# A graph attention layer on one core: the node table in two float32r parts instead of three bfloat16 parts, and one-hot rows made by VectorE

## The chip, the cores and the metric

The kernel runs on one core of a Trainium2 chip. The metric is the device time of one execution in microseconds (us), here the median of three runs. The core has TensorE (PE), VectorE (DVE), ScalarE (ACT), GpSimd (POOL) and SyncE (SP), each with a queue of its own that is worked off in order. SBUF is the working memory with 128 partitions, PSUM takes what TensorE computes. Indirect transfers (gathers and scatters by a list of row numbers) are issued by GpSimd, the others here by SyncE.

## What is computed

12500 nodes of 32 values, 400000 edges sorted by their destination. Two layers follow each other. Cut to what matters:

```python
# layer 0: messages from an edge network and the source's features, summed by destination
x = silu(silu(edge_radial @ W1 + b1) @ W2 + b2);  tpw = x @ W3 + b3
messages = concatenate([m0, m1])        # products of h[src], edge_sh and tpw
agg = segment_sum(messages, dst, num_segments=n_atoms) / sqrt(16)
x = layernorm(x + h_self + agg)
# layer 1: attention
s_src = h @ attn_w[:d];  s_dst = h @ attn_w[d:]
e = s_src[src] + s_dst[dst];  e = where(e >= 0, e, 0.01 * e)
ex = exp(e - segment_max(e, dst)[dst])
out = segment_sum(h[src] * (ex / denom[dst])[:, None], dst)
x = layernorm(x + out)
```

## The kernel before

The edges lie in 3125 tiles of 128, one edge of each tile per partition. Four stages follow each other.

1. The message stage, layer 0. 130 iterations of four groups of six tiles, and a rest. GpSimd gathers the source rows, one indirect transfer per tile (L402). TensorE runs the edge network in float32 (L490, L494, L501), ScalarE the activations, VectorE the products and sums (L808 to L882). In the first 101 iterations one more gather (`dst_row`) serves a search for the edges at which each node's run ends.
2. The node stage. GpSimd gathers 98 columns of sums (`agg0`), VectorE makes the layer norm in seven batches (L1037 to L1052), and after each batch GpSimd scatters 14 columns of attention terms (`starts`, L406), 98 in all. SyncE writes each batch of the new node rows (33 values: 32 features and `s_src`) to `table` in HBM. VectorE also splits each batch into three bfloat16 parts whose sum is the float32 value: high and middle in `xs`, low in `big`.
3. The attention stage, 125 blocks of 25 tiles. The rows of the sources of 20 tiles are gathered by GpSimd from `table`, one transfer of 128 rows each (`gather_block`). Those of the other five tiles are "found" by TensorE: the table lies in SBUF as 128 partitions by 98 nodes, in seven batches of 14 nodes. For each edge a one-hot column says in which partition its source node lies, for each of the seven batches. A matmul of the one-hot rows (128 x 128) with a batch's table part (128 x 462, that is 14 nodes of 33 values) puts the 14 candidates of each edge into PSUM, summed over 7 batches and 3 parts: 21 matmuls per tile, 105 per block (`find_rows`, L536 to L546). VectorE multiplies the 14 candidates by a mask that keeps one (L1079), and sums over them (L1087) into the ring where the gathered rows lie too.
   The one-hot rows are made by ScalarE (`one_hot`, L680 to L697): the square of the difference between the edge's slot number and the partition's (L688), then relu(1 - 2 x square) (L696), for 640 edges at a time and for each batch: 14 instructions per block. There are two copies of them (`hot[k]`), so block b+1's are made while TensorE reads block b's.
   VectorE then does the softmax part of the block (`softmax_block`, L1089 to L1133), with exponentials by ScalarE (L670 to L672), and running sums by scan instructions (L1131); ScalarE lays the result out (L677), SyncE stores it.
4. The last gathers of 98 columns (`agg1`) and the last layer norm.

What orders the attention stage are semaphores. `gather_block(b)` waits until the softmax of block b-2 has used its ring half (`ring_used`) and until the finds of block b-1 are complete (`found_ready`). `find_rows` of a tile waits for the one-hot rows (`hot_ready`) and for VectorE to have multiplied the same PSUM bank of the block before (`found_used`). VectorE's queue has `pick(b)`, then `softmax_block(b)`, which waits for the gathers of block b. Two transposes through TensorE (`turn`) stand ahead of the stage: VectorE needs their results for its last preparations (L1056 to L1065).

## Time and profile before

| | |
|---|---|
| median of three runs | 7700.68 us (7698.39 to 7708.93) |
| span of the profiled execution | 10226.3 us |
| the profiled execution's own time beside its span | the page gives none; the span stands for it |
| granted TensorE clock, mean | 0.737 |
| busy: PE, PE weight loads, DVE, ACT, POOL | 63%, 33%, 49%, 32%, 56% |
| DMA | 331.33 MB, 32 GB/s over the span |

The profiled execution is one run of the program with the hardware profiler on. Its busy shares are of 10226.3 us, not of 7700. "Idle before" in a row is the time for which the engine did nothing ahead of the instructions of that group, and the arrow names what ended it; "issue" means that the profile shows nothing that it waited for. The granted clock is given as a share of full speed: 0.50 is 1.2 GHz, 1.00 is 2.4 GHz. The message stage takes the first half of the span, the attention stage all from about 5370 to 10070 us.

### The profile page before, as it was taken

What the parts mean: (1) busy time and instruction counts of PE and PEld (TensorE: products, weight loads), DVE (VectorE), ACT (ScalarE), POOL (GpSimd) and SP (SyncE); (2) the same over time, 40 slices, a digit from 0 to 9 for tenths busy, and PEclk for the clock granted to TensorE, in tenths of its full rate; (3) what the DMA queues carried; (4) which work ended last, traced back from release to release, by engine and by line L of the source; (5) the groups of instructions that cost most, each with busy time, mean ns of one, the idle gap of its engine ahead of it and who ended that gap; (6) DMA issues with size and microseconds to landing.
All of it is one profiled execution on the core that took longest, in us unless ns stands there. A gap on an engine that the chain in (4) does not pass through costs nothing.

```text
span 10226.3 us, 80982 instructions
## 1 busy us (share of the span) xinstructions
PE 6469.2 (63%) x21671; PEld 3367.5 (33%) x21671; DVE 5013.5 (49%) x8628; ACT 3261.4 (32%) x4929; POOL 5757.4 (56%) x6031
## 2 busy tenths in 40 slices
PE   5666666666666666666516666666666666666662
PEld 3333333433333333434312222222222222222221
DVE  6676666667666666777633222222222222222222
ACT  2323232323323232222203333333333333333330
POOL 6666666666666666666565445555445554445555
PEclk7777777777777777777657777777777777777775
DMA  2111111111111111111101111111111111111111
GB/s 51 37 34 37 35 37 35 37 37 35 37 35 37 35 37 33 29 31 31 40 14 35 29 28 30 31 30 30 30 27 30 31 30 30 29 28 30 30 30 23
DMA packets 338423, 331.33 MB, mean 32 GB/s; under 512 B 184277, under 2 KB 279541, under 8 KB 337859
## 3 DMA queue, kind: packets, MB, share of 16 engines
q0 software_dynamic: 196032, 148.74, 11.5%
q1 hardware_dynamic: 142370, 182.39, 5.7%
q14 instruction: 16, 0.12, 0.0%
q8 instruction: 5, 0.08, 0.0%
HBM read 219.80 MB, written 110.86 MB: 32 GB/s over the span
## 4 chain that ended last, share of the span: by engine, by line
PE 37%; issue 29%; another core or an unknown queue 18%; ACT 7%; DVE 6%; DMA 1%; SPq 1%; ACTq 0%; POOL 0%; DVEq 0%; POOLq 0%
PE tpw L545 25%; PE hid L545 6%; ACT early L570 2%; PE hid L490 2%; ACT hid L564 2%; PE hid L494 2%; PE tpw L501 2%; DVE msgs L882 1%; DVE prod L817 1%; DVE red L829 1%; DVE early L829 1%; ACT hv L577 1%; ACT junk_row L593 1%; ACT early L581 1%
## 5 line engine op out<-in xcount | busy, mean ns | idle before, releaser
L402 POOL DMA_INDIRECT early<-in_x_wide,idx x3126 | 2991.1, 957 | 1919.2 <-DVE prod L817 988.5
L402 POOL DMA_INDIRECT prod<-table,idx x2500 | 2374.1, 950 | 2305.4 <-PE hid L545 1568.4
L545 PE MATMUL tpw<-xs,early 128*128 128x462 bf16 x7000 | 2221.3, 393 | 1048.5 <-issue 1038.5
L501 PE MATMUL tpw<-w3s,early 128*128 128x256 f32 x6252 | 2039.0, 492 | 54.5 <-DVE prod L817 53.8
L501 PEld LDWEIGHTS tpw<-w3s,early 128*128 128x128 f32 x6252 | 1521.3, 252 | 761.9 <-issue 353.9
L545 PE MATMUL tpw<-big,early 128*128 128x462 bf16 x3500 | 1383.6, 395 | 586.6 <-issue 585.9
L494 PE MATMUL hid<-hid,w2s 128*128 128x384 f32 x1044 | 633.2, 699 | 1742.4 <-ACT hid L564 1108.6
L1079 DVE TENSOR_TENSOR prod<-tpw,mask 128x462 f32<-128x462 f32 x500 | 319.8, 640 | 2729.9 <-remote 2185.4
L570 ACT ACTIVATE early<-hid,b2s 64x384 f32<-64x384 f32 x1044 | 602.3, 577 | 2905.0 <-remote 1857.9
L545 PEld LDWEIGHTS tpw<-xs,early 128*128 128x128 bf16 x7000 | 702.3, 101 | 2031.0 <-issue 1454.4
L808 DVE TENSOR_TENSOR prod<-tpw,early 128x1152 f32<-128x1152 f32 x521 | 704.7, 1353 | 886.0 <-remote 813.7
L670 ACT ACTIVATE tpw<-diff 128x25 f32<-128x25 f32 x125 | 24.4, 195 | 2623.5 <-DVE prod L1105 1268.0
L494 PEld LDWEIGHTS hid<-hid,w2s 128*128 128x128 f32 x1044 | 233.7, 253 | 1884.1 <-ACT hid L564 1198.1
L688 ACT ACTIVATE early<-early,bases 128x640 f32<-128x640 f32 x875 | 710.4, 827 | 21.4 <-issue 0.2
L545 PEld LDWEIGHTS tpw<-big,early 128*128 128x128 bf16 x3500 | 362.2, 103 | 1062.1 <-issue 787.1
L817 DVE TENSOR_TENSOR prod<-tpw,hv 128x1152 f32<-128x1152 f32 x521 | 701.3, 1346 | 0.0
L696 ACT ACTIVATE early<-early,bases 128x640 bf16<-128x640 f32 x875 | 700.0, 814 | 0.0
L490 PE MATMUL hid<-early,w1s 16*128 16x384 f32 x1046 | 666.0, 727 | 19.4 <-DMA early<-in_radial_t 10.5
L545 PE MATMUL hid<-xs,early 128*128 128x462 bf16 x1750 | 582.3, 420 | 0.2 <-issue 0.2
L617 ACT ACTIVATE sums<-msgs 128x768 f32<-128x768 f32 x131 | 274.5, 2095 | 652.2 <-DVE msgs L882 412.5
L790 DVE TENSOR_TENSOR bprod<-hv,big 128x288 f32<-128x288 f32 (+1 forms) x261 | 118.5, 454 | 648.8 <-ACT hv L577 407.4
L1087 DVE TENSOR_REDUCE prod<-prod 128x33 f32<-128x462 f32 x625 | 379.7, 624 | 0.0
(176 smaller groups left out, 5718.0 us busy)
## 6 DMA issues: line engine op xcount, KB each, us to landing
scan<-prod SPq DMA_DIRECT2D x125, 425.0 KB
early<-in_x_wide,idx POOLq DMA_INDIRECT x3126
scan<-sums SPq DMA_DIRECT2D x130, 384.0 KB
early<-qrows SPq DMA_DIRECT2D x126, 320.0 KB
prod<-table,idx POOLq DMA_INDIRECT x2500
early<-in_radial_t SPq DMA_DIRECT2D x262, 48.0 KB
big<-in_sh SPq DMA_DIRECT2D x131, 48.0 KB
idx<-in_src SPq DMA_DIRECT2D x262, 6.0 KB
```

The costliest lines, as they stand in the source:

```text
L402: return pool.indirect_dma_start(out=dest, out_offset=None, in_=source, in_offset=bass.IndirectOffsetOnAxis(ap=index, axis=0))
L490: pe.matmul(hid[:, 0, 0:HC], w1s[:, :], rad[:, k, :], start=True, stop=True).then_inc(layers_done, 1)
L494: pe.matmul(hid[:, 1, 0:HC], w2s[:, :], hid1[:, :], start=True, stop=True)
L501: mm = pe.matmul(tpw_v(b)[:, t, :], hid2[:, b, at:at + P], w3s[:, :], start=True, stop=True)
L545: mm = pe.matmul(found[i][:, 0:BC], hot[k][:, g, i * P:(i + 1) * P], split(s, g), start=g == 0 and s == 0, stop=g == NBATCH - 1 and s == S ...
L570: act.activation(hid2[0:HR, b, half * HC:(half + 1) * HC], hid[units, 1, 0:HC], ACT.Silu, bias=b2s[units, :])
L688: act.activation(near[g % 2], qb[k], ACT.Square, bias=near_bias[:, g:g + 1])\
L696: act.activation(hot[k][:, g, :], near[g % 2], ACT.Relu, scale=-2.0, bias=one)\
L808: dve.tensor_tensor(prod_a[b].rearrange("p (t w u) -> p t w u", t=GT, w=MUL), w[:, :, 0:3 * MUL * MUL].rearrange("p t (w u) -> p t w u", w ...
L817: dve.tensor_tensor(prod_b[b].rearrange("p (t i w u) -> p t i w u", t=GT, i=3, w=MUL), w[:, :, 3 * MUL * MUL:].rearrange("p t (w u) -> p t ...
L1079: dve.tensor_tensor(picked[i % 2], found[i][:, 0:BC].rearrange("p (w a) -> p w a", a=BJ), mask[:, k, i:i + 1, :].to_broadcast([P, TW, BJ]) ...
L1087: dve.tensor_reduce(ring[:, k, GT1 + i, :], picked[i % 2], AX, ALU.add).then_inc(picked_ready, 1)
```

## The change

- The table parts are two float32r tensors, `highs` and `lows`: the value rounded to float32r, and the rest. A tile needs 14 matmuls, a block 70.
- The one-hot rows are float32r too, made by VectorE: one comparison of the slot numbers with the partition's number (`is_equal`) per batch. There is one copy of them, in two pieces: tiles 0 to 2 (384 edges) and tiles 3 and 4 (256 edges). Each piece has a semaphore of its own. VectorE makes the first piece for block b+1 in `pick(b)` after the third tile's reduction, the second at the end of `pick(b)`; each waits until TensorE has finished with the piece (`found_ready`).
- ScalarE's one-hot instructions are gone.
- The first block's one-hot rows are made by VectorE right ahead of the loop; TensorE does its two transposes first and has one block per turn of its loop instead of two.
- Buffers of the first half (`xs`, `early`, `hid1` and others) share their places with those of the second (`lows`, `highs`, `hot`, `qb`). The slot numbers are computed in a late part of `big`, and SyncE waits for their store before it goes on.

```diff
-SPLITS = 3
+CHUNKS = ((0, (PT + 1) // 2), ((PT + 1) // 2, PT))
+SPLITS = 2
+BANKS = 5
...
+            lows = sb2("lows", [P, NJ * TW], F32R)
+            highs = sb2("highs", [P, NJ * TW], F32R)
+            hot_f = sb2("hot", [P, NBATCH * PC], F32R)
+            qb = [sb2(f"qb{i}", [P, PC]) for i in range(2)]
...
+        def split(s, g):
+            return (highs, lows)[s][:, g * BC:(g + 1) * BC]
+
+        def hot(c):
+            first_tile, end_tile = CHUNKS[c]
+            return hot_f[:, NBATCH * P * first_tile:NBATCH * P * end_tile].rearrange("p (g e) -> p g e", g=NBATCH)
...
             sp.dma_start(qrows, row_q).then_inc(qrows_out, 16)
+            sp.wait_ge(qrows_out, 16)
...
-                sp.wait_ge(near_ready, b * NBATCH + NBATCH)
+                sp.wait_ge(hot_ready[1], b + 1)
...
-                pool.wait_ge(found_ready, b * PT + 2 * PT)
+                pool.wait_ge(found_ready, b * PT + PT)
...
-            def find_rows(b, k):
-
-                pe.wait_ge(hot_ready, b * NBATCH + NBATCH + 2)
-                for i in range(PT):
-                    pe.wait_ge(found_used, b * PT + i + 1)
-                    for g in range(NBATCH):
-                        for s in range(SPLITS):
-                            mm = pe.matmul(found[i][:, 0:BC], hot[k][:, g, i * P:(i + 1) * P], split(s, g),
-                                           start=g == 0 and s == 0, stop=g == NBATCH - 1 and s == SPLITS - 1)
-                    mm.then_inc(found_ready, 1)
+            def find_rows(b):
+
+                for c, (first_tile, end_tile) in enumerate(CHUNKS):
+                    pe.wait_ge(hot_ready[c], b + 1)
+                    for i in range(first_tile, end_tile):
+                        before = BANKS if i >= BANKS else PT if i >= PT - BANKS else PT - BANKS
+                        pe.wait_ge(found_used, b * PT + i + 1 - before + PT)
+                        at = (i - first_tile) * P
+                        for g in range(NBATCH):
+                            for s in range(SPLITS):
+                                mm = pe.matmul(found[i % BANKS][:, 0:BC], hot(c)[:, g, at:at + P], split(s, g),
+                                               start=g == 0 and s == 0, stop=g == NBATCH - 1 and s == SPLITS - 1)
+                        mm.then_inc(found_ready, 1)
 
             pe.wait_ge(splits_ready, NBATCH)
-            find_rows(0, 0)
             turn(hid[0:1, 1, 0:P], filled[:, T - 1:T], P)
             turn(hid[:, 1, 0:1], cr[2][0:1, :], 1)
-            with pe.Fori(0, PAIRS) as pair:
-                for k in (1, 0):
-                    find_rows(pair * 2 + 2 - k, k)
+            with pe.Fori(0, BLOCKS) as b:
+                find_rows(b)
...
-                hi, mid, lo = (split(s, b).rearrange("p (w j) -> p w j", j=BJ) for s in range(SPLITS))
-                rest = picked[0]
+                hi, lo = (split(s, b).rearrange("p (w j) -> p w j", j=BJ) for s in range(SPLITS))
                 link(dve.tensor_copy(hi, whole))
-                link(dve.tensor_tensor(rest, whole, hi, ALU.subtract))
-                link(dve.tensor_copy(mid, rest))
-                dve.tensor_tensor(lo, rest, mid, ALU.subtract).then_inc(splits_ready, 1)
+                dve.tensor_tensor(lo, whole, hi, ALU.subtract).then_inc(splits_ready, 1)
...
+            def one_hot(b, n, k, c):
+
+                first_tile, end_tile = CHUNKS[c]
+                if c == 0:
+                    dve.wait_ge(qb_in[k], n * 16 + 16)
+                dve.wait_ge(found_ready, b * PT + end_tile)
+                for g in range(NBATCH):
+                    ins = dve.tensor_scalar(hot(c)[:, g, :], qb[k][:, first_tile * P:end_tile * P],
+                                            slot_of[:, g:g + 1], None, ALU.is_equal)
+                ins.then_inc(hot_ready[c], 1)
...
                     dve.wait_ge(found_used, b * PT + PT + i + 1)
                     dve.tensor_reduce(ring[:, k, GT1 + i, :], picked[i % 2], AX, ALU.add).then_inc(picked_ready, 1)
+                    if i + 1 == CHUNKS[0][1]:
+                        one_hot(b + 1, n + k, 1 - k, 0)
+                one_hot(b + 1, n + k, 1 - k, 1)
```

VectorE's queue in one block of the attention loop, from the third tile's reduction to the softmax, in the kernel before (`prod` holds the masked candidates and the ring, `mask` and `tpw` or `hid` are the mask and the PSUM banks):

```order
L1087 TENSOR_REDUCE prod<-prod 128x33 [waits found_used]
L1076 REGISTER_ALU
L1078 REGISTER_ALU [waits found_ready]
L1079 TENSOR_TENSOR prod<-hid,mask 128x462 [waits picked_ready]
L1086 REGISTER_ALU
L1087 TENSOR_REDUCE prod<-prod 128x33 [waits found_used]
L1086 REGISTER_ALU
L1087 TENSOR_REDUCE prod<-prod 128x33 [waits found_used]
L1093 ISA
L1094 REGISTER_ALU [waits ring_in0]
```

The same stretch of the changed kernel, with its own line numbers (`qb` holds the slot numbers, `hot` the one-hot rows):

```order
L1083 TENSOR_REDUCE prod<-prod 128x33 [waits found_used]
L1057 ISA
L1058 ISA [waits qb_in1]
L1060 TENSOR_SCALAR hot<-qb,bases 128x384 [waits found_ready]
L1060 TENSOR_SCALAR hot<-qb,bases 128x384 x6
L1072 REGISTER_ALU
L1074 REGISTER_ALU [waits found_ready]
L1075 TENSOR_TENSOR prod<-hid,mask 128x462 [waits picked_ready]
L1083 TENSOR_REDUCE prod<-prod 128x33 [waits found_used] x2
L1058 REGISTER_ALU
L1060 TENSOR_SCALAR hot<-qb,bases 128x256 [waits found_ready]
L1060 TENSOR_SCALAR hot<-qb,bases 128x256 x6
```

Fourteen compares stand in VectorE's queue now, seven ahead of the last tile's mask multiply and seven ahead of the softmax.

TensorE's queue at the entry of the stage before, the last matmuls of the first block's finds and what follows:

```order
L545 MATMUL hid<-xs,early 128x462 x2
L545 MATMUL hid<-big,early 128x462
L522 MATMUL hid<-ident,big 1x128 [waits to_pe]
L522 MATMUL hid<-ident,cr 128x1 [waits to_pe]
L553 UNCONDITIONAL_BRANCH
L553 ISA
L542 ISA [waits hot_ready]
```

And in the changed kernel, from the node stage's last matmuls on:

```order
L542 MATMUL hid<-wselfs,big 128x32 x2
L531 MATMUL hid<-ident,big 1x128 [waits to_pe,splits_ready]
L531 MATMUL hid<-ident,cr 128x1 [waits to_pe]
L564 UNCONDITIONAL_BRANCH
L564 ISA
L553 ISA [waits hot_ready0]
L557 MATMUL tpw<-highs,hot 128x462 [waits found_used]
L557 MATMUL tpw<-lows,hot 128x462
```

The first block's finds stood ahead of the two transposes; they stand behind them now, and behind VectorE's first compares.

## Rows read from the trace of the kernel before

**Rows 1.** The page: span, and part 1 (busy us, share of the span, instructions).

```profile
span 10226.3 us, 80982 instructions
```

**Rows 2.** Page, costliest groups: busy us, mean ns | idle before, releasers; GpSimd's gathers.

```profile
L402 POOL DMA_INDIRECT early<-in_x_wide,idx x3126 | 2991.1, 957 | 1919.2 <-DVE prod L817 988.5
L402 POOL DMA_INDIRECT prod<-table,idx x2500 | 2374.1, 950 | 2305.4 <-PE hid L545 1568.4
```

**Rows 3.** Timeline (start us, us, instruction, idle before), GpSimd, a block's first gathers.

```profile
7028.81 0.95 POOL L402 DMA_INDIRECT prod<-table,idx  x1 [12.33 <-PE hid L545]
7030.06 0.95 POOL L402 DMA_INDIRECT prod<-table,idx  x1 [0.30 <-issue]
```

**Rows 4.** Windows: busy us (x started) of five engines; TensorE clock, DMA share, GB/s.

```profile
7000.00:7005.00 5.00, 4.83 (x24) 2.13 (x22) 0.00 (x0) 4.94 (x8) 3.78 (x5) 1.00 0.64 161
7005.00:7010.00 5.00, 0.90 (x2) 0.29 (x3) 0.00 (x0) 4.90 (x7) 3.78 (x5) 0.81 0.16 18
...
7020.00:7025.00 5.00, 5.00 (x14) 1.95 (x15) 2.36 (x4) 0.00 (x0) 0.00 (x0) 0.50 0.00 0
7025.00:7030.00 5.00, 5.00 (x27) 2.48 (x26) 1.76 (x4) 0.00 (x0) 0.95 (x1) 0.98 0.00 0
```

**Rows 5.** Timeline, TensorE, two matmuls that are three apart in its queue.

```profile
7026.43 0.36 PE L545 MATMUL hid<-big,early 128*128 128x462 bf16 x1
...
7027.02 0.36 PE L545 MATMUL hid<-big,early 128*128 128x462 bf16 x1
```

**Rows 6.** VectorE, attention stage: groups by line, then a softmax's timeline.

```profile
L1087 DVE TENSOR_REDUCE prod<-prod 128x33 f32<-128x462 f32 x606 | 368.2, 624 | 0.0
...
L1079 DVE TENSOR_TENSOR prod<-tpw,mask 128x462 f32<-128x462 f32 x486 | 311.0, 640 | 2683.2 <-remote 2146.1 <-issue 266.4 <-PE tpw L545 255.6
...
7029.97 0.20 DVE L1095 TENSOR_TENSOR score<-prod,big 128x25 f32<-128x25 f32 x1 [0.16 <-DVE prod L1087]
...
7033.07 2.10 DVE L1131 TENSOR_TENSOR_SCAN msgs<-msgs,tpw 128x150 f32<-128x150 f32 x6
```

**Rows 7.** Page, costliest groups, ScalarE's one-hot instructions.

```profile
L688 ACT ACTIVATE early<-early,bases 128x640 f32<-128x640 f32 x875 | 710.4, 827 | 21.4 <-issue 0.2
...
L696 ACT ACTIVATE early<-early,bases 128x640 bf16<-128x640 f32 x875 | 700.0, 814 | 0.0
```

**Rows 8.** Timeline, TensorE, six float32 matmuls in the message stage.

```profile
1999.88 2.86 PE L501 MATMUL tpw<-w3s,early 128*128 128x256 f32 x12
```

**Rows 9.** Timeline, VectorE, tensor-scalar instructions on float32 in SBUF.

```profile
50.91 0.49 DVE L758 TENSOR_SCALAR early<-amod 128x625 f32<-128x625 f32 x1
...
5228.64 1.79 DVE L1013 TENSOR_SCALAR big<-keep 128x3125 f32<-128x3125 f32 x1
```

**Rows 10.** Timeline, two long VectorE instructions and the gathers beside them.

```profile
5414.49 1.91 DVE L1060 TENSOR_SCALAR msgs<-dstf,carry 128x3125 f32<-128x3125 f32 x1
5416.43 3.42 DVE L1061 TENSOR_TENSOR big<-big,msgs 128x3125 f32<-128x3125 f32 x1
...
5414.65 2.56 POOL L402 DMA_INDIRECT prod<-table,idx  x1 [0.30 <-issue]
5417.51 3.15 POOL L402 DMA_INDIRECT prod<-table,idx  x1 [0.30 <-issue]
```

**Rows 11.** Groups by line, scatters, 5236 to 5310 us, then 5310 to 5366.

```profile
L406 POOL DMA_INDIRECT starts<-tval,start_i x50 | 55.3, 1106 | 50.0 <-DVEq L1045 35.0 <-issue 14.9
...
L406 POOL DMA_INDIRECT starts<-tval,start_i x44 | 42.8, 974 | 13.4 <-issue 13.4
```

**Rows 12.** Timeline, last scatter, and VectorE's steps from there to the loop.

```profile
5365.12 0.97 POOL L406 DMA_INDIRECT starts<-tval,start_i  x1 [0.30 <-issue]
...
5379.42 6.67 DVE L1056 TENSOR_TENSOR_SCAN big<-keep,big 128x3125 f32<-128x3125 f32 x1 [69.28 <-issue]
5412.77 0.28 DVE L969 COPY cr<-hid 1x128 f32<-1x128 f32 x1 [26.68 <-PE hid L522]
...
5420.43 2.12 DVE L1064 MEMSET msgs<- 128x2475 f32 x1 [0.58 <-DVE big L1061]
```

More of the change, by code:

```diff
@@ L11 @@
 BF16 = mybir.dt.bfloat16
+F32R = mybir.dt.float32r
 P = 128
@@ L53 @@
 BC = BJ * TW
-SPLITS = 3
+CHUNKS = ((0, (PT + 1) // 2), ((PT + 1) // 2, PT))
+SPLITS = 2
+BANKS = 5
 ROUND = 12582912.0
-assert NBATCH * BJ == NJ and BC <= 512 and PT <= 5
+assert NBATCH * BJ == NJ and BC <= 512 and BC % 2 == 0 and BANKS <= PT <= 2 * BANKS
 TPAD = (ITERS + 1) * SLOTS * GT
@@ L226, in build, with sb1, sb2 @@
                   for i in range(2)]
+        with ExitStack() as first:
+            def sb1(name, shape, dt=F32):
+                return first.enter_context(nc.sbuf_tensor(name, shape, dt))
+            xs_f = sb1("xs", [P, max(NJ * TW, FIRSTS)])
+            early = sb1("early", [P, rows_end + NC * MUL * CT + FIRSTS // 2])
+            hid1 = sb1("hid1", [P, HC])
+            hv = sb1("hv", [P, 2, HALF * GT, 3 * MUL])
+            bprod = sb1("bprod", [P, HALF * GT, 3, MUL])
+            red_0 = sb1("red", [P, NC, MUL, CT])
+            tmp = sb1("tmp", [P, 3, MUL, CT])
+            keep8 = sb1("keep8", [P, 2, PIECE * CT])
+            junk_row = sb1("junk_row", [P, ROW])
+            dst_row = sb1("dst_row", [P, ROW], I32)
+        with ExitStack() as second:
+            def sb2(name, shape, dt=F32):
+                return second.enter_context(nc.sbuf_tensor(name, shape, dt))
+            lows = sb2("lows", [P, NJ * TW], F32R)
+            highs = sb2("highs", [P, NJ * TW], F32R)
+            hot_f = sb2("hot", [P, NBATCH * PC], F32R)
+            qb = [sb2(f"qb{i}", [P, PC]) for i in range(2)]
+        xs = xs_f[:, NJ * (TW - D):NJ * TW].rearrange("p (j d) -> p j d", d=D)
+        assert all((b + 1) * BC <= NJ * (TW - D) + (b + 1) * BJ * D for b in range(NBATCH))
+        result = xs_f[:, 0:NJ * D].rearrange("p (j d) -> p j d", d=D)
+        firsts = xs_f[:, 0:FIRSTS].bitcast(I32)
+        rad = early[0:2 * NB, 0:SLOTS * HC].rearrange("p (k c) -> p k c", k=SLOTS)
+        hid2 = early[:, SLOTS * HC:2 * SLOTS * HC].rearrange("p (b c) -> p b c", b=2)
+        rows = early[:, 2 * SLOTS * HC:rows_end].rearrange("p (k t c) -> p k t c", k=SLOTS, t=GT)
+        early_red = early[:, rows_end:rows_end + NC * MUL * CT].rearrange("p (c w t) -> p c w t", c=NC, w=MUL)
+        red = [red_0, early_red]
+        junk = early[:, rows_end + NC * MUL * CT:].bitcast(BF16)
+        def split(s, g):
[3 more added lines that the diff above has]
+            return hot_f[:, NBATCH * P * first_tile:NBATCH * P * end_tile].rearrange("p (g e) -> p g e", g=NBATCH)
         hid = pb("hid", [P, 2, 512])
@@ L678, in rows_out @@
                    .then_inc(run_ready, 1)
-            def one_hot(b, pair, k):
-                act.wait_ge(qb_in[k], pair * 16 + 16)
-                act.wait_ge(found_ready, b * PT + PT)
-                def nearness(g):
-                    n = b * NBATCH + g
-                    act.wait_ge(hot_ready, n + (2 if g == 0 else 1))
-                    act.activation(near[g % 2], qb[k], ACT.Square, bias=near_bias[:, g:g + 1])\
-                       .then_inc(near_ready, 1)
-                nearness(0)
-                for g in range(NBATCH):
-                    if g + 1 < NBATCH:
-                        nearness(g + 1)
-                    act.wait_ge(near_ready, b * NBATCH + g + 1)
-                    act.activation(hot[k][:, g, :], near[g % 2], ACT.Relu, scale=-2.0, bias=one)\
-                       .then_inc(hot_ready, 1)
-            one_hot(0, 0, 0)
             with act.Fori(0, PAIRS) as pair:
                 for k in range(2):
-                    one_hot(pair * 2 + k + 1, pair + k, 1 - k)
                     exponents(pair * 2 + k, k)
@@ L1133, in softmax_block @@
                 ins.then_inc(scanned1, 1)
+            for c in range(2):
+                one_hot(0, 0, 0, c)
             with dve.Fori(0, PAIRS) as pair:
                 for k in range(2):
-                    pick(pair * 2 + k, k)
+                    pick(pair * 2 + k, pair, k)
                     softmax_block(pair * 2 + k, pair, k)
-            pick(BLOCKS - 1, 0)
+            pick(BLOCKS - 1, PAIRS, 0)
             softmax_block(BLOCKS - 1, PAIRS, 0)
@@ L1232 @@
         w_self[at, at] = get["L0_gnn_Wv"]
-    base = np.zeros((P, 1 + BJ + NBATCH + 1), np.float32)
+    base = np.zeros((P, 1 + BJ + NBATCH), np.float32)
     base[:, 0] = [p * T for p in range(P)]
     base[:, 1:1 + BJ] = range(BJ)
-    base[:, 1 + BJ:1 + BJ + NBATCH] = [[-(p * NBATCH + g) for g in range(NBATCH)] for p in range(P)]
-    base[:, -1] = 1.0
+    base[:, 1 + BJ:1 + BJ + NBATCH] = [[p * NBATCH + g for g in range(NBATCH)] for p in range(P)]
     nodes = np.array([[p * NJ - 0.5 + j for j in range(-1, SEARCHES)] for p in range(P)], np.float32)
```

77 lines of the change are left out of this document (22 added, 55 removed).

## The prediction, made before the changed kernel was run

> **What bounds the kernel now.** Read the size of the profiled execution first: its span is 10226.3 us [rows 1], while the runs without a profile have a median of 7700.7 us. The page gives no other time for the profiled execution, so its span is what I can add up, and the 2525.6 us between the two must be explained before any edit is priced.
>
> Then read the costliest groups by engine, and of each the idle time before it. GpSimd issues all indirect transfers. Before the node gathers of the first layer it sat 988.5 us for VectorE, and before those of the attention stage 1568.4 us for TensorE [rows 2], in sum 2556.9 us. Take those two waits out and the span becomes 7669.4 us, 31.3 us (0.4%) under the median. So the runs that are timed hold hardly any of them. What is left of GpSimd is a metronome: each gather 0.95 us and 0.30 us to the next, 1.25 us apart [rows 3]. A block of the attention stage has 20, that is 25.0 us; 125 blocks are 3130 us.
>
> Why the profiled execution waits is visible in short windows [rows 4]: TensorE starts 24 or 27 matmuls in 5 us in one window, and 2 in another, with no engine named. The three-part matmuls need 0.59 us for three, 0.197 us each [rows 5], 105 of them 20.7 us, yet GpSimd's busy and idle time before the 2500 node gathers, 4679.5 us [rows 2], make 37.4 us for each of the 125 blocks. The slow issue accounts for the excess; the sum above says that it belongs to the profiled execution. I don't know its cause.
>
> So per block: GpSimd 25.0 us; TensorE 20.7 us, some 2.5 more when it starts at 1.2 GHz (granted clock 0.50, then 0.98 five us later [rows 4]); VectorE, one mask multiply and one reduction per tile, 5 x (0.64 + 0.62) = 6.3 us, and the softmax part from 7029.97 to 7035.17, 5.2 us, about 12 in all [rows 6]; ScalarE 14 one-hot instructions of 0.82 us, 11.4 us, beside its part of the softmax [rows 7]. GpSimd is the bound, TensorE next, 2 to 4 us behind.
>
> **The change part by part.**
>
> Matmuls. 105 become 70 per block. No row has a float32r matmul. From below: the bf16 one of the same shape, 0.197 us, so 13.8 us. From above: a float32 matmul is two instructions, 0.238 us each for 256 columns [rows 8], 0.43 us at 462 columns. I take 0.197, the row with the same shape and one pass; the float32 row pays for passes that one float32r product doesn't have. Gain on the path: 0, because GpSimd's 25.0 us hide it. The cover goes at 25.0 / 70 = 0.36 us per matmul.
>
> One-hot rows. ScalarE loses 14 instructions per block, 11.4 us, off the path: 0. VectorE gets 14 compares, 7 of 384 and 7 of 256 elements. A tensor-scalar instruction took 0.49 us for 625 elements and 1.79 for 3125 [rows 9], so 0.52 ns per element and 0.165 us fixed: 0.365 and 0.298 us, 4.6 us per block. At the rate of the two-input instruction (3.42 us for 3125 elements, rows 10) it would be 7.2. VectorE goes from 12 to between 17 and 19 us, below 25.0: 0 for its time as such.
>
> The new wait. There is one copy of the one-hot rows, in two pieces, where there were two copies. TensorE's first piece of the next block waits for VectorE to take tile 3, reduce tile 2 and make 7 compares: 0.64 + 0.62 + 2.6 = 3.9 us after tile 3 is found. TensorE has tile 4 to do, 2.8 us, so it idles 1.1 us. Queued behind the compares on VectorE are tile 4 and the softmax; they wait for gathers anyway. The loop TensorE-VectorE comes to 13.8 + 1.1 + 2.5 = 17.4 us, under 25.0: 0. SyncE's load of the next row now waits for the second piece instead of a ScalarE instruction; it is used a block later: 0.
>
> What VectorE does to GpSimd. This isn't in the diff. A gather issued at 5414.65, while a tensor-scalar instruction of 1.91 us was running, took 2.56 us, and the next, beside a two-input one of 3.42 us, 3.15 us; each ended 0.81 us after the VectorE instruction did [rows 10]. Undisturbed it takes 0.95. So a gather has one moment near its start at which it waits for a running instruction of this kind. The compares are of this kind and on SBUF on both sides; ScalarE's instructions were not on VectorE at all, and the tile multiplies and reductions leave the gathers at 950 ns on average [rows 2]. Per block, 4.6 us of compares meet 4.6 / 1.25 = 3.7 gathers. From above, at half an instruction each: 3.7 x 0.17 = 0.62 us, 78 us over 125 blocks. From below: 0, since the first layer's gathers, beside many two-input instructions, average 957, 7 ns more. Between them: scatters beside VectorE instructions of 0.62 us took 1.106 us, and 0.974 with VectorE idle [rows 11]: 0.132 us each, scaled by 0.33 / 0.62 it is 0.07 us. I take that: 3.7 x 0.07 = 0.26 us per block, **+32 us**.
>
> The Trainium skill ("SBUF — State Buffer", "Who interferes with whom") says that a copy or tensor-scalar instruction in a 2-port mode holds a port pair shared with GpSimd exclusively, and fully blocks it. By rows 10 the trace agrees that it blocks. If seven compares without a wait between them hold the pair as one, the price is that of the second rival below.
>
> Entry of the stage. Before, the first block's one-hot rows and finds were made during the scatters; TensorE had them in its queue ahead of two transposes. Now the compares stand behind VectorE's last preparations. With the last scatter's end as zero (5366.1): the scan starts at 13.3 [rows 12] and takes 6.7; about 0.6 for the transpose that cost 26.7 in the profile behind TensorE's slow finds; then from 5412.77 to 5422.55, 9.8. That is 30.4. Now 7 compares (2.6), and 70 matmuls, 13 at 0.385, the low clock, as the 14 in 5 us of [rows 4], and 57 at 0.197 (16.2): the first find is complete at 49.2. The gathers of the second block wait for it and would be due at 25.3: 23.9 us late, once. Before, the third block's gathers, due at 50.4, waited for finds that began at 30.4 + 0.9 and took 20.7 + 2.5: 54.5, so 4.1 late. Net **+20 us** (ends: 15, if the clock is high at once, and 30 if it stays low).
>
> The splitting of the table loses two of four VectorE instructions per batch; scatters of 1.28 us, 14 a batch, cover it: 0. The other buffer places and SyncE's early wait for the stored rows: 0, one wait of a few us while GpSimd is busy.
>
> Sum: profiled span without the two waits 7669.4, to the median 31.3, plus 20 plus 32: **7753 us**, 0.7% slower.
>
> **The rivals.**
>
> *TensorE's relief shows (ends faster).* The 31 us over 7669 may be GpSimd waiting for finds in the timed runs too, since TensorE was only 2 to 4 us behind. With 14.9 us of work it would be 10 behind, and they go: 7669 + 20 = 7689 without the compares' effect, and less if the entry costs less than 20. It decides once the sum of those two terms is below the waits that go, about 31 us. For it: TensorE's small reserve. Against: at most 31 us are there, and part of them lies around the span. Faster by over 0.2% 0.10, within 0.2% 0.16. (0.2%, 15 us, is about what a measurement of this kernel tells from no change.)
>
> *The compares block as one run.* The instructions overlap by some 0.08 us when nothing stands between them (six scans in 2.10 us, rows 6), so the runs last 2.0 and 1.6 us; each catches a gather, on average 0.63 us after its start: 1.4 + 1.0 = 2.4 us per block, 300 us: 8050 us. For it: no wait stands between the seven. Against: in rows 10 the gather got through at 40 ns between two instructions. 0.12.
>
> *TensorE becomes the bound.* At the low clock, 0.385 us per matmul, 70 take 27.0 us: 2.0 more than GpSimd, 250 us, 8000 with the two terms. At the float32 instruction's rate, 30.1 us: 5.1 x 125 = 640, 8390. For it: no row of float32r, and idle stretches of TensorE get longer (10 us per block), after which it starts at half clock. Against: in [rows 4] the clock was back at 0.98 within 5 us of steady work, and each find has 14 us of it. 0.08.
>
> The forecast itself, both terms between their ends, 7717 to 7810: 0.54.
>
> **The numbers.** Low end 7690: the first rival with the entry paid. High end 7970: it leaves out the blocked run and most of the slow TensorE, together under 0.2 with what lies below. Faster 0.10, same 0.16, slower 0.54 + 0.12 + 0.08 = 0.74.
>
> **What the profile after would show.** 70 float32r matmuls per block about 0.197 us apart where TensorE isn't held up (0.36 or more: third rival). Compares of 0.36 and 0.30 us; 0.56 and 0.43 would mean the slower mode. Gathers beside compares longer than 0.95 us, mean of the stage near 0.96 (950 would refute the 32 us, 1.06 the mild form). GpSimd waiting about 24 us once before the second block's gathers. ScalarE without the 1750 one-hot instructions. The profiled span itself falls well below 10226, since 140 instead of 210 TensorE instructions per block meet the slow issue, while the timed runs do not get faster: that would be the sharpest sign. I'd be wrong if the timed median fell by more than 31 us: then TensorE was on the path of the timed runs and the sum that takes both waits out was a coincidence.

## The result, and the profile after

The changed kernel took 7731.5 us (median of 5 runs, 7728.3 to 7743.5), the kernel before 7699.8: a ratio of 1.0042, 95% interval 1.003 to 1.0055. It is 0.4% slower. 7753 us had been forecast, in a range of 7690 to 7970.

The profiled execution of the changed kernel took 7743.5 us, with a span of 7741.7. From its page, the span, GpSimd's two groups of gathers (they answer to [rows 1, 2]), and the first group of the new matmuls; columns as there:

```profile
span 7741.7 us, 70937 instructions
...
L411 POOL DMA_INDIRECT early<-in_x_wide,idx x3126 | 3020.8, 966 | 957.1 <-issue 890.3
L411 POOL DMA_INDIRECT prod<-table,idx x2500 | 2398.8, 960 | 773.5 <-issue 761.4
L557 PE MATMUL tpw<-highs,hot 128*128 128x462 f32 x3500 | 1483.1, 424 | 1007.5 <-DVE hot L1060 1007.5
```

The two long waits of [rows 2] are gone, that of the first layer too, whose code did not change. The comparison is with a second profiled execution of the kernel before, which took 7696.6 us (it is the first experiment below). Its gathers, by line:

```profile
L402 POOL DMA_INDIRECT early<-in_x_wide,idx x3126 | 3014.9, 964 | 956.7 <-issue 891.7 <-DMA idx<-in_src 35.5 <-DVE prod L817 29.6
L402 POOL DMA_INDIRECT prod<-table,idx x2500 | 2368.9, 948 | 761.8 <-issue 757.0 <-PE hid L545 4.3 <-PE tpw L545 0.3
```

Set the attention gathers side by side: busy 2398.8 against 2368.9 us, idle 773.5 against 761.8, together 41.6 us more. First layer: 6.3 us more in this execution, none in a second one (below). So the whole loss is in the 2500 gathers of the attention stage, and has two parts: each is 12 ns longer on average, and there is one wait. The wait, in the timeline of GpSimd, with one row of VectorE:

```profile
4403.75 0.97 POOL L415 DMA_INDIRECT starts<-tval,start_i  x1 [0.31 <-issue]
4405.03 0.99 POOL L411 DMA_INDIRECT prod<-table,idx  x1 [0.30 <-issue]
...
4412.82 6.67 DVE L1041 TENSOR_TENSOR_SCAN big<-keep,big 128x3125 f32<-128x3125 f32 x1 [122.69 <-DMA big<-starts]
4413.84 6.40 POOL L411 DMA_INDIRECT prod<-table,idx  x1 [0.31 <-issue]
...
4438.49 0.95 POOL L411 DMA_INDIRECT prod<-table,idx  x1 [0.30 <-issue]
4450.86 0.95 POOL L411 DMA_INDIRECT prod<-table,idx  x1 [11.42 <-PE hid L557]
```

The last scatter, the first gather of the stage, one gather that took 6.40 us because VectorE's long scan ran beside it, and the second block's first gather, 11.4 us late for TensorE's first find. No later gather in the stage waits: all other gaps are 0.30 us. What TensorE did before that moment:

```profile
4432.83 0.75 PE L557 MATMUL tpw<-highs,hot 128*128 128x462 f32 x1 [11.20 <-DVE hot L1060]
4433.38 0.59 PE L557 MATMUL tpw<-lows,hot 128*128 128x462 f32 x1
4433.76 0.59 PE L557 MATMUL tpw<-highs,hot 128*128 128x462 f32 x1
...
4438.33 0.37 PE L557 MATMUL tpw<-lows,hot 128*128 128x462 f32 x1
4438.54 0.37 PE L557 MATMUL tpw<-highs,hot 128*128 128x462 f32 x1
4438.75 0.37 PE L557 MATMUL tpw<-lows,hot 128*128 128x462 f32 x1
```

It waited 11.2 us for VectorE's compares, then ran at 0.385 us per matmul for 4.8 us, then at 0.210. The 12 ns, in a later block (VectorE and GpSimd):

```profile
6025.51 2.40 DVE L1060 TENSOR_SCALAR hot<-qb,bases 128x384 fp32r<-128x384 f32 x7
6025.80 0.94 POOL L411 DMA_INDIRECT prod<-table,idx  x1 [0.30 <-issue]
6027.05 1.02 POOL L411 DMA_INDIRECT prod<-table,idx  x1 [0.30 <-issue]
6027.83 0.62 DVE L1075 TENSOR_TENSOR prod<-hid,mask 128x462 f32<-128x462 f32 x1
```

Beside the seven compares one gather keeps its 0.94 us and the next takes 1.02. And windows of the block before it (busy us and starts of TensorE, its weight loads, VectorE, ScalarE, GpSimd; clock, DMA share, GB/s; they answer to [rows 4]):

```profile
6000.00:6005.00 5.00, 2.37 (x6) 2.12 (x7) 5.00 (x15) 0.00 (x0) 3.78 (x5) 0.50 0.44 80
6005.00:6010.00 5.00, 5.00 (x19) 4.35 (x19) 1.12 (x4) 0.00 (x0) 3.78 (x5) 0.71 0.15 14
6010.00:6015.00 5.00, 5.00 (x25) 4.47 (x24) 0.00 (x0) 0.00 (x0) 3.78 (x5) 1.00 0.14 13
6015.00:6020.00 5.00, 5.00 (x24) 4.16 (x23) 3.51 (x15) 1.10 (x3) 3.78 (x5) 1.00 0.18 17
6020.00:6025.00 5.00, 0.05 (x1) 0.00 (x0) 4.81 (x12) 1.73 (x1) 3.78 (x5) 1.00 0.34 90
```

GpSimd is busy 3.78 us of every 5, which is its full rate (four gathers of 1.25). TensorE rests 8 us per block (1007.5 us over 125) and begins each find at the half clock, 1.2 GHz (0.50 in the first window, 1.00 in the third). What the change saved on it has become idle time.

### The profile page after: what moved, and what is told of

Read it like the earlier page. It is cut to its first block, busy times and chain, and to the rows that moved or that the text cites. A ratio compares the mean times of both kernels' runs of the same rounds, so it can differ in the third digit from the quotient of the medians.

```text
span 7741.7 us, 70937 instructions
## 1 busy us (share of the span) xinstructions
PE 4979.6 (64%) x17296; PEld 3662.1 (47%) x17296; DVE 5520.8 (71%) x10378; ACT 1937.9 (25%) x3179; POOL 5816.2 (75%) x6031
## 4 chain that ended last, share of the span: by engine, by line
POOL 50%; issue 26%; DVE 10%; DMA 6%; ACT 4%; SPq 1%; PE 1%; POOLq 0%; DVEq 0%; ACTq 0%
POOL prod L411 30%; POOL early L411 16%; DMA early<-in_x_wide,idx 3%; POOL msgs L411 3%; ACT sums L627 2%; DVE red L817 2%; DVE prod L805 2%; DVE msgs L870 2%; DMA early<-in_radial_t 1%; POOL starts L415 1%; DVE early L817 1%; DVE prod L796 1%; PE hid L499 1%; ACT hv L587 1%; DMA idx<-in_src 1%
## 5 line engine op out<-in xcount | busy, mean ns | idle before, releaser
L411 POOL DMA_INDIRECT prod<-table,idx x2500 | 2398.8, 960 | 773.5 <-issue 761.4
L557 PE MATMUL tpw<-highs,hot 128*128 128x462 f32 x3500 | 1483.1, 424 | 1007.5 <-DVE hot L1060 1007.5
L510 PE MATMUL tpw<-w3s,early 128*128 128x256 f32 x6252 | 1817.4, 450 | 96.0 <-DVE prod L805 95.0
L510 PEld LDWEIGHTS tpw<-w3s,early 128*128 128x128 f32 x6252 | 1367.1, 226 | 679.4 <-issue 271.4
L557 PE MATMUL tpw<-lows,hot 128*128 128x462 f32 x3500 | 1444.3, 413 | 0.0
L557 PEld LDWEIGHTS tpw<-highs,hot 128*128 128x128 f32 x3500 | 769.0, 220 | 1155.5 <-issue 1055.4
L503 PE MATMUL hid<-hid,w2s 128*128 128x384 f32 x1044 | 538.8, 604 | 1057.6 <-ACT hid L574 1057.6
L557 PEld LDWEIGHTS tpw<-lows,hot 128*128 128x128 f32 x3500 | 764.4, 218 | 92.0
L1060 DVE TENSOR_SCALAR hot<-qb,bases 128x384 fp32r<-128x384 f32 x1764 | 562.3, 387 | 0.2 <-DVE prod L1050 0.2
L499 PEld LDWEIGHTS hid<-early,w1s 16*128 16x128 f32 x1046 | 179.8, 214 | 518.5 <-DMA early<-in_radial_t 291.8
L823 DVE TENSOR_REDUCE red<-prod 128x144 f32<-128x1152 f32 x261 | 350.9, 1344 | 0.0
```

The costliest lines, as they stand in the source:

```text
L411: return pool.indirect_dma_start(out=dest, out_offset=None, in_=source, in_offset=bass.IndirectOffsetOnAxis(ap=index, axis=0))
L499: pe.matmul(hid[:, 0, 0:HC], w1s[:, :], rad[:, k, :], start=True, stop=True).then_inc(layers_done, 1)
L503: pe.matmul(hid[:, 1, 0:HC], w2s[:, :], hid1[:, :], start=True, stop=True)
L510: mm = pe.matmul(tpw_v(b)[:, t, :], hid2[:, b, at:at + P], w3s[:, :], start=True, stop=True)
L557: mm = pe.matmul(found[i % BANKS][:, 0:BC], hot(c)[:, g, at:at + P], split(s, g), start=g == 0 and s == 0, stop=g == NBATCH - 1 and s == S ...
L823: return dve.tensor_reduce(red[m][:, 3:NC, :, tiles].rearrange("p i w t -> p t (i w)"), prod_b[k % 2].rearrange("p (t i u) -> p t i u", t= ...
```

## The experiments

Theory 1: GpSimd's gathers pace the kernel, so less work on TensorE and ScalarE gives nothing; the loss is the late entry plus the delay of gathers by VectorE's compares. Its rivals: the 12 ns come from the float32r matmuls or the buffers' new places; or the loop of VectorE and TensorE paces the blocks.

**The kernel before, once more.** No edit.

> The kernel before, unchanged, for a second profiled execution. Theory 1 (GpSimd paces; the slow issue belongs to the one profiled execution): span about 7698 us; TensorE without idle time that no engine ends; gathers of the first layer mean 966 ns as in the changed kernel (the 957 of the first profile came from its waits), gathers of the attention stage mean 950; GpSimd waits about 4 us for TensorE at the third block's gathers and nowhere else in that stage. Rival (TensorE still paces some blocks before): GpSimd waits for finds in many blocks, 30 us in sum. Rival (the slow issue belongs to this kernel under the profiler): span again over 9000 us.

Measured: span 7694.8 us, no idle time of TensorE that no engine ends, gathers of 964 and 948 ns (rows above). The 4.3 us put down to TensorE are gaps of 0.30 us that are there anyway, at the starts of blocks: in the whole stage no gap is longer than 0.4 us. The rival with 30 us of hidden waits falls, and the other with it.

**One-hot rows on ScalarE, float32r kept.**

```diff
+                    def nearness(g):
...
+                        act.activation(near[g % 2][:, 0:size], qb[k][:, first_tile * P:end_tile * P], ACT.Square,
+                                       bias=slot_of[:, g:g + 1]).then_inc(near_ready, 1)
...
+                        act.activation(hot(c)[:, g, :], near[g % 2][:, 0:size], ACT.Relu, scale=-2.0, bias=one)\
+                           .then_inc(hot_ready, 1)
...
-                    if i + 1 == CHUNKS[0][1]:
-                        one_hot(b + 1, n + k, 1 - k, 0)
-                one_hot(b + 1, n + k, 1 - k, 1)
```

> The changed kernel with the one-hot rows made by ScalarE again, by its square and its clamp (28 instructions per block, in the two pieces), with the float32r table, the single copy of the one-hot rows and the new buffer places kept. Theory 1: attention gathers back to a mean of 950 ns, -25 us; the first block's rows are ready before VectorE's last preparations, so that its finds start some 11 us earlier and the wait of 11.4 us goes: 7731 - 25 - 11 = 7695 us, the time of the kernel before. Rival 2 (float32r matmuls or the buffer places cost it): 7731 - 11 = 7720, mean 960. Rival 3 (ScalarE, 28 instructions of about 0.5 us, becomes what the blocks wait for): over 7800.

Measured: 7699.1 us, against 7699.7 for the kernel before in the same comparison: ratio 0.9999 (0.999 to 1.0008). By line:

```profile
L413 POOL DMA_INDIRECT prod<-table,idx x2500 | 2371.1, 948 | 761.6 <-issue 761.0 <-DMA scan<-prod 0.3 <-PE hid L559 0.3
```

948 ns, and no wait. All of the loss goes with the place of the one-hot work; the float32r table, the single copy of the one-hot rows and the overlaid buffers cost nothing that shows, and a third fewer matmuls bring nothing. The rivals on the 12 ns fall. This run undoes the entry's delay as well, so it does not divide the loss between the two terms.

**The entry alone put back.**

```diff
             pe.wait_ge(splits_ready, NBATCH)
+            find_rows(0)
             turn(hid[0:1, 1, 0:P], filled[:, T - 1:T], P)
...
-            with pe.Fori(0, BLOCKS) as b:
-                find_rows(b)
+            with pe.Fori(0, BLOCKS - 1) as b:
+                find_rows(b + 1)
```

VectorE's `one_hot(0, 0, 0, c)` for both pieces stands ahead of `dve.wait_ge(fill_in, 16)` here.

> The changed kernel with the first block's compares ahead of VectorE's wait for the scattered starts, and its finds ahead of TensorE's two transposes, as the kernel before had them; the loop unchanged. Theory 1: the wait of 11.4 us before the second block's gathers goes, the 960 ns of the gathers stay: 7720 us. Rival (entry costs nothing, all of the 31.7 us is in the loop): 7731. Rival (entry costs the 20 us predicted): 7711.

Measured: 7725.3 us, ratio 1.0032 (1.002 to 1.0044). The trace:

```profile
L411 POOL DMA_INDIRECT prod<-table,idx x2500 | 2396.0, 958 | 761.8 <-issue 761.1 <-PE hid L557 0.3 <-DMA scan<-prod 0.3
```

The wait is gone from the idle time (761.8 again) and the gathers stay at 958 ns. So 25.6 us over the kernel before, or 26.2 over the run with ScalarE, is what the compares in the loop cost. The 5 us above the expected 7720 are taken up next.

**The changed kernel, once more.** No edit.

> The changed kernel, unchanged, for a second profiled execution, since its first was its slowest run (7743 us, median 7731). 7731 us; GpSimd again waits 11.4 us for TensorE once, at the second block's gathers. If that wait were shorter here (5 us), it would explain why undoing the entry gave back 6.2 us and not 11.

Measured: 7735.3 us, ratio 1.0052 (1.0038 to 1.0065); the wait is 11.0 us, as in the first profile. So the entry's price in the trace is 11 us. In the timed medians it is 6 or 10 us, depending on which of the two medians of the changed kernel one takes (12, if each kernel is taken against the kernel before of its own comparison: 37.3 less 25.6); with five runs each the medians do not tell these apart.

**Every compare twice.**

```diff
                     ins = dve.tensor_scalar(hot(c)[:, g, :], qb[k][:, first_tile * P:end_tile * P],
                                             slot_of[:, g:g + 1], None, ALU.is_equal)
+                    if not isinstance(b, int):
+                        dve.tensor_scalar(again[:, g, 0:(end_tile - first_tile) * P],
+                                          qb[k][:, first_tile * P:end_tile * P],
+                                          slot_of[:, g:g + 1], None, ALU.is_equal)
```

> The changed kernel with every one-hot compare of the loop made a second time, into a buffer that nobody reads: 14 more compares per block, 4.6 us of VectorE. Theory 1 (compares delay the gathers they meet; VectorE's time as such is hidden): another 10 ns on each of the 2500 attention gathers, +25 us, 7756 us; gather mean 970 ns. Rival 2 (the 10 ns come from something else, as the buffers' new places or the float32r matmuls): no change, 7731, mean 960. Rival 3 (the loop of VectorE and TensorE paces the blocks): the 4.6 us show in each of 125 blocks, up to +575 us, 8300. Rival 4 (compares block as one run): +300 us.

Measured: 7751.0 us, ratio 1.0066 (1.0052 to 1.008): 16 to 20 us over the changed kernel. Attention gathers and a few rows of a block:

```profile
L413 POOL DMA_INDIRECT prod<-table,idx x2500 | 2407.5, 963 | 773.1 <-issue 760.9 <-PE hid L559 11.8 <-DMA scan<-prod 0.3
```

```profile
6007.48 0.94 POOL L413 DMA_INDIRECT prod<-table,idx  x1 [0.30 <-issue]
6007.73 0.34 DVE L1062 TENSOR_SCALAR hot<-qb,bases 128x256 fp32r<-128x256 f32 x1
6007.99 0.55 DVE L1065 TENSOR_SCALAR again<-qb,bases 128x256 fp32r<-128x256 f32 x1
6008.46 0.34 DVE L1062 TENSOR_SCALAR hot<-qb,bases 128x256 fp32r<-128x256 f32 x1
6008.71 0.34 DVE L1065 TENSOR_SCALAR again<-qb,bases 128x256 fp32r<-128x256 f32 x1
6008.72 0.95 POOL L413 DMA_INDIRECT prod<-table,idx  x1 [0.30 <-issue]
```

VectorE's added 4.6 us per block, 575 us in all, are hidden: rivals 3 and 4 fall. But the gathers grew by 4 ns, not 10. The price does not grow in proportion. In this block the 256-element compares leave the gathers at 0.94 and 0.95 us, and it is one of the compares that takes 0.55 us instead of 0.34.

**Narrower compares.** That row suggested that only the 384-element ones delay.

```diff
-                for g in range(NBATCH):
-                    ins = dve.tensor_scalar(hot(c)[:, g, :], qb[k][:, first_tile * P:end_tile * P],
-                                            slot_of[:, g:g + 1], None, ALU.is_equal)
+                for g in range(NBATCH):
+                    for at in range(first_tile, end_tile, 2):
+                        to = min(at + 2, end_tile)
+                        ins = dve.tensor_scalar(hot(c)[:, g, (at - first_tile) * P:(to - first_tile) * P],
+                                                qb[k][:, at * P:to * P], slot_of[:, g:g + 1], None, ALU.is_equal)
```

> The changed kernel with each compare of 384 elements made as one of 256 and one of 128: 7 more instructions per block, 1.2 us more of VectorE, the same elements. In the changed kernel gathers beside the 384-element compares are delayed (1.02 and 1.12 us for 0.944), those beside the 256-element ones are not. Theory 1a (a gather waits for the rest of a running compare beyond some length): the delays go, mean 946 ns, -25 us: 7706 us. Theory 1b (the delay goes with the time or the elements of the compares): as before or a little more, 7731 to 7738, mean 960. Rival (the compares have nothing to do with it): 7731.

Measured: 7747.2 us, ratio 1.0062 (1.0049 to 1.0076), 12 us slower than the changed kernel in the same comparison:

```profile
L411 POOL DMA_INDIRECT prod<-table,idx x2500 | 2408.6, 963 | 773.0 <-issue 761.2 <-PE hid L557 11.4 <-DMA scan<-prod 0.3
```

```profile
6028.65 2.05 DVE L1062 TENSOR_SCALAR hot<-qb,bases 128x256 fp32r<-128x256 f32 x7
6029.01 1.05 POOL L411 DMA_INDIRECT prod<-table,idx  x1 [0.30 <-issue]
```

Theory 1a is refuted: here a gather beside 256-element compares takes 1.05 us. The traces of the changed kernel had refuted it already. In its second profile 71 gathers beside the 256-element compares took over 0.97 us, one of them this:

```profile
5363.76 1.91 DVE L1060 TENSOR_SCALAR hot<-qb,bases 128x256 fp32r<-128x256 f32 x7
5363.92 1.87 POOL L411 DMA_INDIRECT prod<-table,idx  x1 [0.30 <-issue]
```

What the traces suggest is that the delay depends on where in a gather a compare ends. In the first profile of the changed kernel 638 gathers ran beside compares, and 248 of them took over 0.97 us. Every one of these 248 ended 0.78 to 0.85 us after the end of some compare, the distance at which the two gathers in [rows 10] ended after longer instructions. So a gather mostly waits for the rest of a compare that already runs, and not for the seven. Where the compares fall shifts with everything ahead of them. This is not the whole rule. With seven tiles (below) 246 of 497 lengthened gathers ended about 0.91 us after a compare. And the gather of 1.87 us above, with six others of 1.87 to 1.89 in that profile, each beside seven 256-element compares, ended 0.12 us after the last of the seven, so these were held for all that was left of the run; twelve of 1.67 to 1.68 us in this experiment's profile ended likewise.

**Six and seven tiles on TensorE.** If GpSimd paces, TensorE's new idle time is worth as many gathers as fit into it.

```diff
-PT = 5
+PT = 6
```

> The changed kernel with 6 of each block's 25 tiles found by TensorE (84 float32r matmuls, 14 compares of 384) and 19 gathered. If GpSimd sets the pace: 1.252 us less per block, 125 blocks: -156, so 7575 us. If TensorE or VectorE sets it: 7731 or slower.

Measured: 7595.0 us, ratio 0.9867 (0.9852 to 0.9882), 20 us above the 7575 expected. With PT = 7:

> The changed kernel with 7 tiles found by TensorE (98 matmuls at 0.210 us are 20.6 us per block, with some 2.5 for the half clock at their start) and 18 gathered (22.5 us). GpSimd sets the pace: -313, so 7418 us, up to 7440 with compares of 512 and 384 elements. Rival, TensorE's 23.1 us now pace the block, 0.6 over GpSimd: 7418 + 75 = 7493. Rival, VectorE's chain of picks, compares and softmax, 20 us, in series with TensorE's find: over 7600.

Measured: 7498.4 us, ratio 0.9742 (0.9727 to 0.9757): the fastest of all kernels here, 2.6% under the kernel before. The attention gathers of the two, by line:

```profile
L411 POOL DMA_INDIRECT prod<-table,idx x2375 | 2287.9, 963 | 737.1 <-issue 720.7 <-PE tpw L557 16.1 <-DMA scan<-prod 0.3
```

```profile
L411 POOL DMA_INDIRECT prod<-table,idx x2250 | 2219.9, 987 | 702.4 <-issue 657.6 <-PE tpw L557 44.5 <-DMA scan<-prod 0.3
```

GpSimd paces at both. It waits for TensorE once, at the entry, 13.6 us with six tiles and 17.1 with seven; the rest of the 16.1 and 44.5 us is its usual gap of 0.30 us, and no other gap in the stage is longer than 0.4 us. The seventh tile gives 97 us instead of 156. The time, 58 us over the upper end of the 7418 to 7440 expected, is near the one that was worked out for TensorE as the bound (7493), but comes another way: the gathers take 987 ns, 39 more than the 948 undisturbed, 88 us over 2250.

**The same with one-hot rows on ScalarE.** The edit of the second experiment, with PT of 6 and 7; its two work buffers lie in the ends of `msgs` and `sums` here.

> Six of 25 tiles on TensorE, the one-hot rows made by ScalarE. 7698 - 125 x 1.25 = 7542 us, gathers at 946 ns, no wait for TensorE in the loop. Rival (ScalarE in the chain): 7595 or more.

Measured: 7548.0 us, ratio 0.9807 (0.979 to 0.9823), gathers at 949 ns: 47 us better than six tiles with VectorE's compares, and 6 us off the sum.

> Seven of 25 tiles on TensorE, as in seven_on_tensor, but the one-hot rows made by ScalarE (28 instructions per block, of 512 and 384 elements, some 17.5 us). If the excess of 84 us on the gathers there comes from VectorE's compares, and the waits of 44.5 us for finds from the late entry and the compares in the loop, both go: attention gathers mean 946 ns, 7498 - 84 - 27 = about 7387 us (by another way, the kernel before less 250 gathers of 1.25 us: 7698 - 312 = 7386). Rival: ScalarE's 20.3 us per block in series with TensorE's find exceed GpSimd's 22.5 us: GpSimd waits in every block, 7500 or more.

Measured: 7576.2 us, ratio 0.9843 (0.9826 to 0.9859): the rival. The gathers are undisturbed at 948 ns, but GpSimd now waits for finds at the start of 82 of 125 blocks, 181 us in sum beyond its usual gaps. (The 27 us of waits in the loop that the expectation took off never existed, as said above.) By line, then what seems to hold the finds up, in ScalarE's and VectorE's timeline of one block:

```profile
L414 POOL DMA_INDIRECT prod<-table,idx x2250 | 2133.3, 948 | 866.5 <-issue 649.3 <-PE tpw L560 204.4 <-DVE tpw L1129 12.5
```

```profile
6005.73 0.60 ACT L710 ACTIVATE hot<-msgs,bases 128x384 fp32r<-128x384 f32 x1
6006.23 0.17 ACT L683 ACTIVATE tpw<-diff 128x25 f32<-128x25 f32 x1
6006.44 1.19 DVE L1129 TENSOR_TENSOR tpw<-tpw,prod 128x200 f32<-128x200 f32 x4 [5.41 <-ACT tpw L683]
```

VectorE's softmax waited 5.4 us for an exponential of 0.17 us, queued on ScalarE behind the last one-hot instruction.

**Six tiles with a third product.** The low product is added twice; the values found are not the table's.

```diff
-                            for s in range(SPLITS):
+                            for n, s in enumerate((0, 1, 1)):
...
```

> six_on_tensor with the low product added twice, so three products per slot group instead of two (the second low product is work added; the values found are not the table's): 126 float32r matmuls per block, 26.5 us at 0.210, 1 to 3 us of waits beside them, against GpSimd's 23.8 us. If the saved third product is what makes the sixth tile affordable: TensorE paces, 3.7 to 5.2 us per block over six_on_tensor, 8055 to 8245 us. Rival (TensorE has room anyway): 7595.

Measured: 8038.8 us, ratio 1.0443 (1.0425 to 1.046):

```profile
L411 POOL DMA_INDIRECT prod<-table,idx x2375 | 2279.2, 960 | 1184.5 <-issue 689.7 <-PE tpw L557 494.7
```

GpSimd now waits for TensorE at every block after the first, 461 us in sum beyond its usual gaps, against 13 us once with two products. Six tiles with three products are 342 us slower than the kernel before, with two 103 us faster. So the third product, at the price of a float32r matmul, is what six tiles can't afford. The kernel before with six tiles in three bfloat16 parts was not run; an estimate from the 0.197 us of [rows 5] is 126 x 0.197 = 24.8 us of TensorE per block, against the 25.0 of its twenty gathers, so next to no gain.

**Seven tiles and the early entry.** The edit of entry_early in seven_on_tensor, with only the first five tiles' finds ahead of the transposes.

> seven_on_tensor (VectorE's compares, 7 of 25 tiles on TensorE) with the entry of entry_early: the first block's compares ahead of VectorE's wait for the scattered starts, and the finds of its first five tiles, for which there are banks, ahead of the two transposes. The wait of 17.1 us before the second block's gathers shrinks to 0 to 4 us, the compares in the loop stay: 7498 - 15 = 7483 us (7478 to 7488). If the entry gives back only part, as in entry_early, 7490.

Measured: 9897.7 us, with the kernel before at 10323.8 in the same comparison, ratio 0.9586 (0.957 to 0.9602). Here the kernel before itself took a third longer than in the other comparisons, as its first profiled execution had, so the 15 us in question can't be read from it and stay open. TensorE's timeline shows how the time is lost, not why:

```profile
7023.71 0.46 PE L557 MATMUL hid<-lows,hot 128*128 128x462 f32 x1 [1.06 <-issue]
7025.83 0.54 PE L557 MATMUL tpw<-highs,hot 128*128 128x462 f32 x1 [1.66 <-issue]
7027.92 0.55 PE L557 MATMUL tpw<-lows,hot 128*128 128x462 f32 x1 [1.55 <-issue]
```

Matmuls 2 us apart, with nothing named that they wait for, in a kernel whose matmuls otherwise stand 0.21 us apart.

## Why the prediction was right, and where it was not

The direction, the bound and the split into two costs were right; the total was 21 us high, most of it in the entry. Two terms came out near by errors that cancelled. Step by step:

- *GpSimd is the bound; TensorE's 35 and ScalarE's 14 saved instructions are worth 0.* Right: one-hot rows back on ScalarE with 70 matmuls give 0.9999 of the time before. The first rival (relief shows) is excluded by the second profile of before, in which no attention gather waits.
- *Take both waits out of the profiled span, add 31.3.* The sum held, for neither of the reasons I left open, and in part by luck. The undisturbed span is 7694.8, with 1.8 us around it, so the sum came out 25.4 us low. With busy and idle time together, the first layer's gathers were 938.7 us shorter in the second profile, where I took out 988.5, and the attention gathers 1548.7 us shorter, where I took out 1568.4; these 69.5 us too much were mostly made up by 44.1 us elsewhere, 40.6 of them at the scatters, that I had not taken out. A part of the 69.5 is that the first layer's gathers were busy for 2991.1 us [rows 2] with the waits and for 3014.9 without them. Most likely a GpSimd that stands waiting is less often beside VectorE's work; then taking a wait out of a span leaves out the contention that the wait had avoided. No run tests this.
- *The slow issue belongs to the profiled execution.* Wrong. It came back in a comparison in which every run, with a profile or without, had it: 10323.8 us. It goes with the chip that comparison ran on or its condition then; with one such comparison that can't be told. So the sign that I called the sharpest, a fall of the profiled span by fewer instructions that meet the slow issue, was no test: the first layer's wait went as well, where no instruction changed.
- *A float32r matmul at 0.197 us.* 0.210, so 14.7 us per block instead of 13.8; of no effect at five tiles.
- *The new wait of TensorE, 1.1 us per block.* 8.1 us. The compares stand behind the softmax on VectorE, and that behind the last gather, so TensorE, once early, idles until there. It cost nothing: no later gather waits.
- *Compares of 0.36 and 0.30 us.* Seven in 2.40 and in 2.08 us: 0.34 and 0.29.
- *What compares do to gathers, 32 us.* 30 us in the traces (11.9 ns on each of 2500: 959.5 ns in the second profile after, 947.6 in that of before), 25.6 in the timed runs of entry_early. The product is right partly by luck, for its factors are not: 3.7 gathers per block at 70 ns were forecast; in the second profile after, of the 2480 gathers after the first block 257 took over 0.97 us, 2.1 per block, at 113 ns more each than 944. That I treated the phase as random was the fault. In the traces the delays fall on about two gathers of every block, nearly all in the same three places in it, and doubling the compares added 9 us of delay (2407.5 against 2398.7 us busy), not 30.
- *The blocked run, 8050 us.* Excluded. The Trainium skill ("SBUF — State Buffer", "Who interferes with whom") has the port pair held exclusively by a tensor-scalar instruction in a 2-port mode, and GpSimd fully blocked. Whether the compares run in such a mode, no profile shows. The trace agrees for a single long instruction ([rows 10], and in the first profile after a gather of 2.00 us that ended 0.12 us after a tensor-scalar instruction of 1.91). For the run it mostly doesn't: the mean gather grew by 12 ns, most of the lengthened ones waited for the rest of one compare, and a compare sometimes gives way instead. But seven gathers of 2480 in the second profile were held to the end of a run of seven, at 1.87 to 1.89 us, and one in compares_twice, at 3.00. The mechanism of this rival exists, then, but is rare.
- *The entry, net 20 us.* 11 us: the term that was mis-sized most. The first find was complete 46.1 us after the last scatter (4450.86 against 4404.72), 49.2 forecast. But the second block's gathers were due at 34.7, not at 25.3: I counted the first block's as 20 x 1.25 us although [rows 10] show two of them stretched to 2.56 and 3.15; the scan stretched another to 6.40. The lateness of 4.1 us at the third block before, which I deducted, did not exist.

With measured terms the sum would have been 7700.7 + 11 + 30 = 7742, against 7731.5 and 7735.3 timed in two comparisons. Of the 6 to 10 us between, some 4 are that the compares cost 25.6 us in the timed runs and 30 in the traces; the rest stays open. For comparison, the profiled pair differs by 38.7 us (7733.5 against 7694.8), the timed one on that chip by 37.3.

## What to carry to other kernels

Work taken off an engine that is not the bound comes back as idle time there, and is worth something only once the bound's work is moved into it: the same change is 0.4% slower at five tiles, and with seven it is 2.6% faster than the kernel before. Before pricing an edit that moves work to VectorE, count the GpSimd transfers that would run beside it, also at the one place where the stage is entered. When a profiled execution is far from the timed runs, take a second profile before building on a difference of the two. And idle time that a row puts down to an engine need not be a wait: 27 of the 44.5 us at seven tiles were gaps that are there anyway.

## What the runs showed of the hardware

- Interference between VectorE and GpSimd is mutual and depends on phase. Of 638 gathers beside compares 248 were lengthened, from 0.94 to between 0.97 and 1.16 us, and each of these ended 0.78 to 0.85 us after a compare's end (first profile after). Seven others of the second profile, at 1.87 to 1.89 us, were held to the end of a run of seven compares. A 256-element compare whose record is 0.34 us long took 0.55 beside a gather. Splitting compares made it worse (12 us).
- Long VectorE instructions of other kinds hold gathers up as well: at the entry of the stage one gather took 6.40 us beside a scan of 6.67, one 2.00 beside a tensor-scalar instruction of 1.91, one 3.85 beside a two-input one of 3.42.
- The same kernel took 7700 us on some chips and 10324 on another, in one comparison, all runs of a comparison alike, with TensorE's matmuls up to 2 us apart and no cause in the trace.
- TensorE's weight loads for float32r took 0.22 us on average in the profile after, for bf16 0.10; matmuls of 462 columns still came every 0.210 us, against 0.197.
- At the stage's entry, after a rest of 11.2 us, TensorE ran 12 matmuls at half clock, 0.385 us each, before it was at 0.210. In the later blocks, after rests of about 8 us, it was 7 to 16 matmuls.
- ScalarE's timeline shows a function table load of 1.28 us once in two blocks, in the kernel before, in the changed one and with one-hot rows back on ScalarE.
